# Attention scores of batches 3 to 7 computed with keys on the output partitions, and turned back

## The reference

```python
kp = k @ Wk.T;  vp = v @ Wv.T + bv;  qp = layernorm(x) @ Wq.T + bq      # k = v = the context
probs = softmax(qp @ kp.T / sqrt(512))                                   # 512 tokens x 77 keys
x = x + tanh(g_xattn) * (probs @ vp @ Wo.T + bo)
xn = fp4(layernorm(x))
h = silu(xn @ fp4(w_gate).T) * (xn @ fp4(w_up).T)
x = x + tanh(g_ffn) * (fp4(h) @ fp4(w_down).T)
```

## Time and profile before

| | |
|---|---|
| median of three runs | 839.90 us (839.57 to 840.34) |
| the profiled execution | 839.68 us, of which the profile's span is 837.9 us |
| TensorE matmuls busy | 833.1 us in 4,208 instructions |
| VectorE busy | 705.4 us in 1,175 |
| ScalarE busy | 378.1 us in 669 |
| GpSimd busy | 366.2 us in 284 |
| DMA queue 1 | 36.3% of 16 engines |
| granted TensorE clock | 1.0 over the span |

### The profile page before, as it was taken

One profiled execution on the slowest core, in us unless ns is written; L12 is line 12 of the kernel. 1 busy time (PEld: TensorE's weight loads), 2 busy tenths in 40 slices (PEclk: granted clock), 3 DMA queues, 4 the chain that ended last, 5 costly groups with the idle time before them and its releaser, 6 DMA issues.

```text
span 837.9 us, 11655 instructions
## 1 busy us (share of the span) xinstructions
PE 833.1 (99%) x4208; PEld 428.6 (51%) x4208; DVE 705.4 (84%) x1175; ACT 378.1 (45%) x669; POOL 366.2 (44%) x284
## 2 busy tenths in 40 slices
PE   9999999999999999999999999999999999999998
PEld 5656556544554445444544444445544454444445
DVE  6797999889988899988897899889887999777754
ACT  2566575834453435434453445335532454333320
POOL 3487464444434344444433543454344424344321
PEclk9999999999999999999999999999999999999999
DMA  9723021063064225422442255224532343222233
GB/s 329 271 74 116 8 60 25 14 131 87 13 135 132 52 58 112 118 58 48 106 120 60 61 110 130 63 61 86 103 67 60 73 92 77 50 56 51 60 72 73
DMA packets 170672, 72.70 MB, mean 87 GB/s; under 512 B 154243, under 2 KB 155893, under 8 KB 170615
## 3 DMA queue, kind: packets, MB, share of 16 engines
q1 hardware_dynamic: 170615, 71.97, 36.3%
HBM read 22.76 MB, written 8.39 MB: 37 GB/s over the span
## 4 chain that ended last, share of the span: by engine, by line
PE 99%; ACT 0%; issue 0%; POOL 0%; DVE 0%; POOLq 0%
PE banks L1819 63%; PE banks L1941 26%; PE banks L1825 2%; PE banks L1813 1%; PE banks L1957 1%; PE banks L1917 1%; PE banks L1882 1%; PE banks L1908 1%; PE banks L1907 1%; PE banks L1838 1%; PE banks L2047 1%; PE banks L2054 0%; PE banks L2064 0%; PE banks L2069 0%; PE banks L2059 0%; PE banks L1883 0%
## 5 line engine op out<-in xcount | busy, mean ns | idle before, releaser
L1819 PE MATMUL banks<-wgu_hi,x_T 128*128 128x512 f16 (+1 forms) x1536 | 440.3, 361 | 0.0
L1819 PE MATMUL banks<-wgu_lo,x_T 128*128 128x512 f16 (+1 forms) x768 | 277.5, 361 | 0.0
L1819 PEld LDWEIGHTS banks<-wgu_hi,x_T 128*128 128x128 f16 x1536 | 150.4, 98 | 153.4 <-issue 0.5
L1941 PE MATMUL banks<-wd,arena 128*128 128x512 f16 x1023 | 226.5, 379 | 0.0
L1941 PEld LDWEIGHTS banks<-wd,arena 128*128 128x128 f16 x1023 | 99.7, 98 | 117.6
L589 POOL TENSOR_TENSOR arena<-arena,h_r 128x1024 f32<-128x1024 f32 (+1 forms) x60 | 92.0, 1534 | 129.5 <-DVE h_r L1234 129.5
L589 POOL TENSOR_TENSOR arena<-arena,h_s 128x1024 f32<-128x1024 f32 x64 | 90.2, 1410 | 85.0 <-DVE arena L1282 43.3
L1819 PEld LDWEIGHTS banks<-wgu_lo,x_T 128*128 128x128 f16 x768 | 75.1, 98 | 76.5 <-issue 0.7
L589 POOL TENSOR_TENSOR xwork<-xwork,x_s 128x512 f32<-128x512 f32 x32 | 37.2, 1164 | 169.2 <-DVE xwork L1282 169.2
L1457 DVE SCALAR_TENSOR_TENSOR arena<-arena,scal,banks 128x512 f32<-128x512 f32 (+1 forms) x90 | 62.6, 697 | 46.2 <-PE banks L1819 44.5
L915 ACT ACTIVATE arena<-banks,scal 128x512 f32<-128x512 f32 (+1 forms) x96 | 61.9, 648 | 82.1 <-PE banks L1819 81.5
(11 more groups left out here) (187 smaller groups left out, 980.3 us busy)
## 6 DMA issues: line engine op xcount, KB each, us to landing
ring<-in_x_dram SPq DMA_DIRECT2D x8, 1024.0 KB, 5.1
out_dram<-ring SPq DMA_DIRECT2D x31, 256.0 KB, 2.0
arena<-in_L_ffn_w_down_dram SPq DMA_DIRECT2D x4, 704.0 KB, 4.0
arena<-in_L_ffn_w_gate_dram SPq DMA_DIRECT2D x5, 512.0 KB, 9.9
arena<-in_L_ffn_w_up_dram SPq DMA_DIRECT2D x5, 512.0 KB, 9.4
ring<-in_L_xattn_Wk_dram SPq DMA_DIRECT2D x4, 256.0 KB, 5.4
ring<-in_L_xattn_Wq_dram SPq DMA_DIRECT2D x4, 256.0 KB, 5.9
wd<-in_ctx_dram SPq DMA_DIRECT2D x1, 1024.0 KB
```

The source lines that it names most:

```text
L1819: ended = e.matmul(at, l, r, start=(i == 0), stop=(i == len(terms) - 1))
L1941: ended = e.matmul(down_ps(t)[:, :], l, r, start=(k == 0 and i == 0), stop=(k == KH - 1 and i == 2))
```

## The change

For batches 3 to 7 the keys become the stationary operand, 77 columns wide, and two token tiles (256 columns) move at a time. `score_pair(b, h)` issues three matmuls for each of the four steps: high keys by high tokens, high keys by low tokens, low keys by high tokens. Pair 0 stands at "a2" and pair 1 at "a3"; nothing is left at "a1". All four tiles' scores of a batch lie in bank 5 as 77 partitions by 512 tokens. `scores_out(b)` on ScalarE, at "a4", brings them to SBUF, multiplies by the scale of the split and adds the bias, which is now one number a partition (`keyb_col`). `score_turn(b)` on TensorE, at "a4", turns them with four f32 transposes into bank 6, with tokens on the partitions. VectorE's `softmax(b)` moves from "soft" to "a4", behind h_round(t, 0), and is only the maximum, read from bank 6; the exponentials read bank 6 and write `prob`. The bias of the second half of the keys is made directly as columns, with 20 products of one moving column, in place of the product of 308 columns. `xnT` becomes one tensor, so that both tiles of a pair can be moved at once, and `xn_turn` waits for the scores of the whole pair that used the buffers before.

```diff
--- before.py
+++ after.py
@@ -94,7 +94,9 @@
         wd_hi = wd[:, 0:KH * D].rearrange("p (k n) -> p k n", k=KH)
         wd_lo = wd[:, KH * D:2 * KH * D].rearrange("p (k n) -> p k n", k=KH)
         keyq = sb("keyq", [P, KD, ROWS])
-        keyb = sb("keyb", [P, ROWS])
+        keyb = sb("keyb", [P, HALF])
+        keyb_col = sb("keyb_col", [P, NBATCH])
         valo = sb("valo", [P, NBATCH, D])
         ident = sb("ident", [P, P])
         neg_ident = sb("neg_ident", [P, P], F16)
@@ -158,7 +160,8 @@
             return h_early[t] if t in h_early else h_buf[t % 2]
 
         xn1 = sb("xn1", [P, TILES, D])
-        xnT = [sb(f"xnT{i}", [P, KD, P]) for i in range(2)]
+        xnT_all = sb("xnT", [P, 2, KD, P])
+        xnT = [xnT_all[:, i, :, :] for i in range(2)]
         prob = sb("prob", [P, TILES, KEYS])
         prob_bytes = sb("prob_bytes", [P, TILES * P])
         probT = prob_bytes[0:KEYS, :]
@@ -173,7 +176,9 @@
 
         CUT = 3
         xn_parts = [xn1[:, i, :].bitcast(F16) for i in range(2)]
-        xn_T = [xnT[i][:, :, :].rearrange("p k n -> p (k n)").bitcast(F16).rearrange("p (k n) -> p k n", k=2 * KD) for i in range(2)]
+        xn_T = xnT_all[:, :, :, :].rearrange("p i k n -> p (i k n)").bitcast(F16).rearrange("p (i k n) -> p i k n", i=2, k=2 * KD)
+        scores_T = xn1[0:KEYS, 2, :]
         CUT_COLS = ROWS - CUT * KEYS
         key_work = [t.bitcast(F16)[:, 0:2 * CUT_COLS] for t in (xn1[:, 2, :], xn1[:, 3, :], prob_bytes[:, :], xn1[:, 2, :])]
         assert CUT > STACKED and 2 * CUT_COLS <= 2 * D
@@ -186,6 +191,8 @@
 
         def cut_tile(b, i):
             return (b - CUT) * TILES + i
+        assert CUT * KEYS <= HALF and (NBATCH - CUT) * KEYS <= ROWS
 
         def xn_there(b, i):
 
@@ -345,6 +352,7 @@
         NTH = {"gu": 1, "d": 2, "v": 3, "k": 4}
         max_turned, pow_spread = sem("max_turned"), sem("pow_spread")
         xn_turned, score_mm, prob_turned, att_mm = (sem(n) for n in ("xn_turned", "score_mm", "prob_turned", "att_mm"))
+        scores_sb, scores_turned = sem("scores_sb"), sem("scores_turned")
         gate_mm, up_mm, down_mm = (sem(n) for n in ("gate_mm", "up_mm", "down_mm"))
 
         x_turned, h_turned, last_turned, p_turned = (sem(n) for n in ("x_turned", "h_turned", "last_turned", "p_turned"))
@@ -504,8 +512,8 @@
             def xn_turn(b, i):
                 m = cut_tile(b, i)
                 w.wait_ge(xn_lo, m + 1)
-                w.wait_ge(score_mm, b * TILES + i - 1)
-                e.dma_start_transpose(xn_T[i % 2][:, :, :], xn_parts[i % 2]).then_inc(xn_moved[i % 2], 16)
+                w.wait_ge(score_mm, b * TILES + i // 2 * 2)
+                e.dma_start_transpose(xn_T[:, i % 2, :, :], xn_parts[i % 2]).then_inc(xn_moved[i % 2], 16)
 
             def turn_part(t, s):
                 b = t // TILES + 1
@@ -844,10 +852,19 @@
                     w.wait_ge(score_mm, n - 1)
                 e.copy(xnT[i % 2][:, :, :], by_k(bank[turn_bank["xn", n]][:, 0:D], KD)).then_inc(xn_sb, 1)
 
+            def scores_out(b):
+                w.wait_ge(score_mm, TILES * (b + 1))
+                w.wait_ge(key_sb, 2 * KEYS_HALF)
+                e.activation(scores_T, bank[5][0:KEYS, 0:TILES * P], ACT.Identity, bias=keyb_col[0:KEYS, b:b + 1],
+                             scale=k_fold[0:KEYS, :]).then_inc(scores_sb, 1)
             def exps(b):
                 w.wait_ge(top_made, b + 1)
+                if b >= CUT:
+                    w.wait_ge(p_lo, b - STACKED)
+                    w.wait_ge(rden_made, b)
                 for i in range(TILES):
-                    e.activation(prob[:, i, :], prob[:, i, :], ACT.Exp, bias=neg_top[:, i:i + 1]).then_inc(exp_done, 1)
+                    e.activation(prob[:, i, :], prob[:, i, :] if b < CUT else bank[6][:, i * KEYS:(i + 1) * KEYS], ACT.Exp, bias=neg_top[:, i:i + 1]).then_inc(exp_done, 1)
 
             def prob_copy(b):
                 w.wait_ge(prob_turned, b + 1)
@@ -860,6 +877,7 @@
                 w.wait_ge(ln1_rstd, b + 1)
                 if m >= 2:
                     w.wait_ge(xn_lo, m - 1)
+                    w.wait_ge(scores_turned, m // TILES)
                 else:
                     w.wait_ge(xn_turned, TILES * CUT)
                     w.wait_ge(k_parts, KD)
@@ -951,6 +969,8 @@
                     xn_apply(b, 3)
                     xn_high(b, 2)
                     xn_high(b, 3)
+                elif b >= CUT and (s, at) == (1, "a4"):
+                    scores_out(b)
                 elif b >= CUT and (s, at) in ((0, "a3"), (0, "a4"), (1, "a2")):
                     return
                 elif (s, at) == (0, "d apply"):
@@ -975,8 +995,12 @@
             def key_copy(i):
                 j, m = divmod(i, KEYS_HALF)
                 w.wait_ge(key_mm, i + 1)
-                to = keyq[:, m, j * HALF:(j + 1) * HALF] if m < KD else keyb[:, j * HALF:(j + 1) * HALF]
-                e.mul(to, bank[mm_bank["key", i]][:, 0:HALF], SOFT).then_inc(key_sb, 1)
+                if m < KD:
+                    e.mul(keyq[:, m, j * HALF:(j + 1) * HALF], bank[mm_bank["key", i]][:, 0:HALF], SOFT).then_inc(key_sb, 1)
+                elif j == 0:
+                    e.mul(keyb[:, :], bank[mm_bank["key", i]][:, 0:HALF], SOFT).then_inc(key_sb, 1)
+                else:
+                    e.mul(keyb_col[0:KEYS, CUT:NBATCH], bank[mm_bank["key", i]][0:KEYS, CUT:NBATCH], SOFT).then_inc(key_sb, 1)
 
             def wo_copy(r):
                 w.wait_ge(wo_turned, r + 1)
@@ -1329,20 +1353,18 @@
 
             def softmax(b):
                 sc = att_ps[:, 0:TILES * KEYS].rearrange("p (i n) -> p i n", i=TILES)
-                kb = keyb[:, b * KEYS:(b + 1) * KEYS].rearrange("p (a n) -> p a n", a=1).broadcast_to([P, TILES, KEYS])
+                kb = keyb[:, b % CUT * KEYS:(b % CUT + 1) * KEYS].rearrange("p (a n) -> p a n", a=1).broadcast_to([P, TILES, KEYS])
+                if b >= CUT:
+                    turned = bank[6][:, 0:TILES * KEYS].rearrange("p (i n) -> p i n", i=TILES)
+                    w.wait_ge(scores_turned, b - CUT + 1)
+                    w.wait_ge(exp_done, TILES * b)
+                    e.tensor_reduce(neg_top[:, :], turned, axis=AX_X, op=ALU.max, negate=True).then_inc(top_made, 1)
+                    return
                 w.wait_ge(key_sb, keys_of(b))
                 w.wait_ge(score_mm, TILES * (b + 1))
                 if 0 < b <= STACKED:
                     w.wait_ge(prob_turned, b)
-                elif b > STACKED:
-                    w.wait_ge(p_lo, b - STACKED)
-                if b < CUT:
-                    e.tensor_tensor(prob[:, :, :], sc, kb, ALU.add).then_inc(score_in, 1)
-                else:
-                    of_parts = banks[:, 5 * BANK:7 * BANK].rearrange("p (i n) -> p i n", i=TILES)
-                    e.scalar_tensor_tensor(prob[:, :, :], of_parts[:, :, 0:KEYS], k_fold, kb, ALU.mult, ALU.add).then_inc(*step())
-                    w.wait_ge(dve_step, step.n)
-                    e.scalar_tensor_tensor(prob[:, :, :], of_parts[:, :, KEYS:2 * KEYS], k_fold, prob[:, :, :], ALU.mult, ALU.add).then_inc(score_in, 1)
+                e.tensor_tensor(prob[:, :, :], sc, kb, ALU.add).then_inc(score_in, 1)
                 w.wait_ge(score_in, b + 1)
                 e.tensor_reduce(neg_top[:, :], prob[:, :, :], axis=AX_X, op=ALU.max, negate=True).then_inc(top_made, 1)
 
@@ -1520,7 +1542,7 @@
                     value_power()
                 elif (s, at) == (1, "a3") and b >= STACKED:
                     value_low(b)
-                elif b >= STACKED and (s, at) == (1, "soft"):
+                elif (s, at) == ((1, "soft") if b < CUT else (1, "a4")) and b >= STACKED:
                     softmax(b)
                 elif b >= STACKED and (s, at) == (1, "d soft"):
                     prob_low(b)
@@ -1871,24 +1893,34 @@
                 turn(turn_bank["xn", n], [xn1[:, i, k * P:(k + 1) * P] for k in range(KD)]).then_inc(xn_turned, 1)
 
             def att_scores(b, i):
-                if b >= CUT:
-                    at = 5 + i // 2
-                    if i % 2 == 0:
-                        take(at, (score_in, b + 1))
-                    w.wait_ge(k_parts, KD)
-                    w.wait_ge(*xn_there(b, i))
-                    c = i % 2 * BANK // 2
-                    for k in range(KD):
-                        e.matmul(bank[at][:, c:c + 2 * KEYS], xn_T[i % 2][:, k, :], key_parts(b, k), start=(k == 0), stop=False)
-                        ended = e.matmul(bank[at][:, c:c + KEYS], xn_T[i % 2][:, KD + k, :], key_parts(b, k)[:, 0:KEYS], start=False, stop=(k == KD - 1))
-                    ended.then_inc(score_mm, 1)
-                    return
                 if i == 0:
                     take(5, (score_in, b + 1))
                 w.wait_ge(key_sb, keys_of(b))
                 w.wait_ge(xn_sb, b * TILES + i + 1)
                 product(att_ps[:, i * KEYS:(i + 1) * KEYS],
```

(39 more changed lines are left out.)

## The result

The changed kernel takes 847.86 us (median of 4 runs, 846.36 to 848.39) where the kernel before takes 839.97 (839.57 to 840.34): ratio 1.0091, 95% interval 1.0074 to 1.0109. It is slower, as forecast, and 0.6 us from the forecast 847.3. That closeness is partly luck: the term for turning back was sized too large, and a fall of TensorE's clock that was not in the sum at all took its place.

The account below looks back on a forecast made before the run. TensorE was taken to bound the kernel: +4.9 us for scores, +1.8 for turning back and +0.7 for key bias make +7.4 on the profiled 839.68, 847.1, or 847.3 us set against the median; range 845.0 to 851.3.

Parts of the forecast that it names:

- What bounds: Whole kernel: TensorE bounds it, its issued work is paid in full; other engines' time costs nothing until TensorE waits.
- Scores: TensorE, batches 3 to 7: 24 matmuls of 256 columns replace 32, 2.62 for 1.64 us a batch, +4.9 us.
- Turning back: TensorE, batches 3 to 7: four added f32 transposes at 0.09 us each, 0.36 us a batch, +1.8 us.
- Key bias: Second half of the keys, once: 40 one-column matmuls, 2.8 us, replace the last key product, 2.1 us: +0.7 us.
- Slack at the transposes: Batch 4, score_turn: ScalarE's eviction of the scores ends 2.6 us before TensorE's transposes need it, so no wait.
- The second pair's transposing DMAs: SyncE's queue, batch 4: transposes of tokens 2 and 3 follow VectorE's low part, so the later wait on scores costs nothing.
- the customers behind the softmax chain: Work waiting on late VectorE, sharpest tile 15's product: 4.5 us of slack against 0.4 net; nothing reaches TensorE.
- VectorE's idle time: VectorE, ahead of the low part of the probabilities: idle 2 to 3 us where it idled 1.03.
- the place of x_apply on ScalarE: ScalarE, batch 4: x_apply taken at its old time plus TensorE's shift of 0.5 us.
- The wait at score_turn: Rival: ScalarE's eviction comes too late for the transposes, TensorE waits 0.8 us a batch, 851.3 us; chance 0.06.
- exposed loads: Rival: none of the 24 narrow score loads a batch hides, each costs 0.06 us, 7.2 us more, 854.5 us; chance 0.03.
- a time that follows the stationary width: Rival: matmul time follows stationary width, 77 of 128, so the kernel is not slower, 840.0 us; chance 0.03.

Follow-up runs that it names:

- where the eviction had no cover: Changed kernel with the four transposes right behind the second pair of tiles, ahead of the down product instead of behind 24 of its matmuls: 864.55 us.
- the two 128-column kernels: Changed kernel with one token tile (128 columns) moving per matmul instead of two: 848.77 us with 77 stationary columns, 847.43 us with 128.
- the one with groups of 8: Changed kernel with the 40 one-column key-bias matmuls in five groups of 8 between weight turns and key products instead of in a row: 846.99 us.
- the trimmed one: Changed kernel with the column matmuls in five groups of 8 and the first half's broadcast key bias cut from 308 to 231 columns: 846.85 us.

## Why the prediction was right

*What bounds.* TensorE is busy throughout the five periods after the change as before, and pays for what it issues; VectorE lost 10.8 us of work with the change, and 5.5 us put back in the experiment did nothing. Right.

*Scores,* +4.9 us: 0.109 us and 2.62 a batch as reckoned. The price goes by the moving columns, since with half of them a matmul takes 0.056. Right.

*Turning back,* +1.8: the mis-sized term, measured +1.35. I took 0.09 between 0.067 and 0.105, since 77 columns lie nearer to 104 than to one; it was 0.067. The transposes of 128 columns in the stream take 0.87 us for eight, 0.109 each, and 77/128 of it is 0.066; the row of one column gave 0.067 as well, so no run here tells whether the columns or a least spacing set it. The four of 104 columns, from which the upper bound came, begin behind a wait, and the difference of their totals is not the spacing in a stream: the four of 77 behind a wait, where the eviction had no cover, would give (0.46 - 0.23)/3 = 0.077 by the same reckoning.

*Key bias,* +0.7: at full clock the chain has +0.69 (the row takes 2.70 us where I reckoned 2.8), so the price was right. But in half the executions the clock falls at the row or behind it, and the profiled one paid 2.35 us in all. I had named a granted clock under 1.00 as a thing that would prove me wrong, and it came true in two of four runs; there was no row for it, since nothing in the trace before has 40 matmuls of one column behind one another. The two errors, 0.45 too much for turning back and nothing for a fall that costs 1.66 in half of the runs, cancel in part, so the median came out near. That is luck.

*Hand-overs.* Slack at the transposes 2.6 us predicted, 3.0 found; no wait. The second pair's transposing DMAs and the customers behind the softmax chain hold as argued. VectorE's idle time was put at 2 to 3 us and is 3.48. The step that failed here, without a price in TensorE's time, is the place of x_apply on ScalarE: I moved it with TensorE's 0.5 us, but it starts 2.0 us later in its period (the last section says why), and the table load comes behind it.

*Rivals.* The wait at score_turn exists only when the cover is taken away; exposed loads, and a time that follows the stationary width, are refuted by the two 128-column kernels. The sum itself closes in the traces. From the first down product to the last group of matmuls of 256 columns (line 1957 before, 1989 after) the kernel before takes 644.90 us, and the changed kernel, the one with the old bias product, the one with groups of 8 and the trimmed one take 651.19 each: +6.29, for 4.9 and 1.35 of the corrected sum. The rest lies ahead of the first down product, at 183.05 us before: 185.34 in the changed kernel (the clock fell), 183.78 with the same row at full clock, 183.68 with groups of 8. With groups of 8 that is 6.3 and 0.6, 6.9 together, its span being 844.8 for 837.9. The medians of the kernels without the row of 40 stand 6.8 to 7.2 us above the kernel before; what is over the sum there is inside the 1.5 us over which the runs of the kernel before spread.

## What to carry to other kernels

Where the chain is one engine for 99% of the span, count what that engine issues: turning a product around so that other engines get a simpler input costs its columns, 6,144 for 3,696 here, and relief elsewhere is worth nothing. A spacing of small matmuls should be taken from a row whose matmuls stand in an unbroken stream. And look twice at a long run of very small matmuls, even where its own time looks harmless: here breaking it up between larger ones cost 0.2 us and kept the clock in every execution.

## What the hardware showed that was not expected

TensorE's clock fell from 2.4 to 1.2 GHz while the engine was busy without a gap: with 40 one-column f32 matmuls in a row (2.70 us at full clock) in 18 of 35 executions, with 80 in all of 4, inside the row, and with groups of 8 in none. What follows pays for it: in the changed kernel 1.81 us for 0.93 and 3.94 for 3.44. The fall need not come in the row. With VectorE's work put back (the maximum taken three times) the row and the transposes still ran at full clock, and the whole price, 1.69 us, fell on the product behind them:

```profile
89.61 2.70 PE banks L2059 x40
92.31 0.93 PE banks L1850 x8
93.24 5.13 PE banks L1844 x8
```

The second surprise is GpSimd. Its two small statistics operations at s = 1 ran beside the softmax before and run beside h_round now, as the softmax left that place. Order of time, the kernel before and the changed one:

```profile
420.62 0.55 POOL L619 TENSOR_TENSOR rstd<-mv,neg_half 128x1 f32<-128x1 f32 x1 [0.18 <-DVE mv L1419]
421.24 0.19 POOL L621 TENSOR_TENSOR shift<-shift,rstd 128x1 f32<-128x1 f32 x1
```
```profile
424.65 1.46 POOL L627 TENSOR_TENSOR rstd<-mv,neg_half 128x1 f32<-128x1 f32 x1 [0.18 <-DVE mv L1441]
426.19 0.82 POOL L629 TENSOR_TENSOR shift<-shift,rstd 128x1 f32<-128x1 f32 x1
```

The first of them, one value a partition, takes 0.55 us beside VectorE operations that read PSUM and 1.46 beside VectorE operations on SBUF alone (424.49 to 426.96), the second 0.19 and 0.82. That is what delays x_apply. Conversely the low part on VectorE fell from 1.37 to 0.48 us: before, GpSimd ran its large multiplication (424.59 to 426.52) at that moment, now it does not. That the two engines exclude each other in SBUF is an inference from these pairs; no experiment was made on it. The Trainium skill (SBUF — State Buffer, "SBUF: two separate sides") says that an operation of VectorE with two SBUF inputs and one of GpSimd that reads SBUF take a shared port pair for a whole instruction, so that the other waits. By that rule h_round (two SBUF inputs) should hold GpSimd up and the old bias operations (one input in PSUM) should not, and both pairs agree, with 1.46 for 0.55 and 1.37 for 0.48 us.
